# Turning attention weights on VectorE by 32x32 blocks instead of on TensorE, in a criss-cross attention kernel

## The chip, the cores and the metric

The kernel runs on one core of one Trainium2 chip. The metric is the device time of one execution in microseconds (us); a smaller one is better. "Profiled execution" means one execution that the hardware profiler recorded.

## The reference

For each of 8 images `x` (512 channels, 96 x 96) every pixel attends to its column and to its row. Cut to what matters:

```python
q = einsum('oc,bchw->bohw', Wq, x) + bq      # 64 channels
k = einsum('oc,bchw->bohw', Wk, x) + bk
v = einsum('oc,bchw->bohw', Wv, x) + bv      # 512 channels
energy_H = einsum('bchw,bcgw->bhwg', q, k) - 1e30 * eye      # along the column, itself masked
energy_W = einsum('bchw,bchv->bhwv', q, k)                   # along the row
att = softmax(concatenate([energy_H, energy_W], -1), -1)
out = gamma * (einsum(v, att_H) + einsum(v, att_W)) + x
```

All of it is float32.

## The kernel before

Each engine has its own program, written out by hand; semaphores order them, and every engine works strictly in the order of its own list. A batch is one image. Its columns and its rows are each cut into 24 chunks of `ROWS` = 4 (4 x 96 = 384 elements). The softmax is applied in two parts: exponentials of each chunk are stored to a scratch in HBM (`e_scratch`), with maxima `mx` and sums `zs` kept apart, and at the end of the energies `factors` works out one multiplier per pixel for columns and one for rows (`F`).

A batch then has two stages.

- **Column stage**, 24 chunks. SyncE loads a chunk of exponentials (`load_p`, 144 KB, into one of three buffers of `Pe`) and two pieces of 384 KB of the input with columns first (`load_xtc`, a ring of 6 pieces, `XT_r` and `XT_c`). GpSimd multiplies the chunk by its factors (`scale`, L390). TensorE turns each of the chunk's four 96 x 96 squares (`turn`, L867) into bank 7, ScalarE copies them to `Pt` (`copy_turned`, L499), and TensorE multiplies the input pieces by them (`attend_column`, L881: 16 products, 32 instructions in the trace). The four columns that come out go to `Y`, two by VectorE (L679), two by ScalarE (L505), each as four copies of 96 elements with a stride.
- **Row stage**. The same for the rows (`attend_row`, L900), whose results VectorE adds to `Y` (`add_row`, L687). Interleaved with it in iterations n = 0 to 23 runs the projection with Wv (`project`, L912, 48 products of 384 columns, the operand split in a high and a low part by `round_y` L516 and `low_y` L616), and VectorE's `finish` (L696) adds the bias and the input again.

Iterations 6 to 17 also carry the projection to q and k and the row energies of the next batch ("A chunks", two an iteration), iterations 18 to 22 its column energies ("B groups", five an iteration). At n = 23 `factors`, `factors_of_columns` and `factors_of_rows` make `F` for the next batch; the factors of rows are turned by TensorE (L861). For one chunk of energies VectorE does a maximum (L625), a subtraction into the ring `E` (L630) and a sum (L639), ScalarE the exponential (L486), GpSimd the mask (L381, columns only), SyncE the store (L217, L222).

A load waits until its buffer is free: `load_p(i)` waits for the turn of chunk i - 3 (semaphore `p_turned`), `load_xtc(i)` for the last product of piece i - 6. In SyncE's list of the column stage they stand as `load_p(g + 4)`, then the two pieces 2g + 6 and 2g + 7.

Of the kernel before, what the change touches and what calls it, by code (L numbers as in the profile page):

```python
# [7 lines left out]
AX_X = mybir.AxisListType.X  # L8
F32 = mybir.dt.float32
# [15 lines left out]
RBANKS = 3  # L25
# [24 lines left out]
def criss_cross_attention(nc, x, x_col, x_row, wqk_t, wv_t, bqk, bv, gamma, out):  # L50
# [8 lines left out]

    e_dram = nc.dram_tensor("e_scratch", (2, B, N, N, N), F32, kind="Internal").ap()  # L60

    ctx = ExitStack()
    with ctx:
# [10 lines left out]
        with ExitStack() as s1:  # L74
            XA = sb("XA", [P, 2, CT, CP], F32, s1)
            Sx = sb("Sx", [P, 2, CT, CP], F32R, s1)
            E = sb("E", [P, ERING, ROWS, N], F32, s1)
            KQ = sb("KQ", [P, POS], F32, s1)
            Kg = sb("Kg", [P, 2, CP], F32, s1)
            st = sb("st", [P, 4, N], F32, s1)  # L80
        with ExitStack() as s2:
# [17 lines left out]
        Pe = sb("Pe", [N, PRING, ROWS, N])  # L99
        Pt = sb("Pt", [P, 2, CP])  # L100
        Q = sb("Q", [P, 2, CP])
        mx = sb("mx", [N, 2, N])
        zs = sb("zs", [N, 2, N])
        F = sb("F", [N, 2, N])
# [6 lines left out]
        oc_ps, or_ps, proj_ps = (*bank[0:3], bank[5]), bank[0:RBANKS], bank[3:5]  # L111
        ec_ps, t_ps = bank[5:7], bank[7]
        st_ps, f_ps = bank[5], bank[6]
# [14 lines left out]
        def turns(a):  # L128
            return 2 if a == 0 else 1

# [18 lines left out]
        f_turned, f_made = sem("f_turned"), sem("f_made")  # L149
        p_in = [sem(f"p_in{j}") for j in range(PRING)]  # L150
        p_scaled, p_turned, pt_made = sem("p_scaled"), sem("p_turned"), sem("pt_made")
# [11 lines left out]
        by_pe = (x_half_used, qk_summed, e_summed, p_turned, o_summed, proj_summed)  # L163
        by_act = (x_hi_made, kq_evicted, q_gathered, e_exped, pt_made, c_moved_act, y_hi_made)
        by_dve = (x_lo_made, e_maxed, e_shifted, z_summed, c_moved_dve, r_added, y_lo_made, out_made, f_made)
# [3 lines left out]
        def past(s, n):  # L169
            return n + START[s]  # L170
# [28 lines left out]
        def _(sp):  # L199
# [15 lines left out]
            def store_row_energies(a, m):  # L215
                sp.wait_ge(e_exped, past(e_exped, e_no(a, m)))
                sp.dma_start(e_dram[1, a, :, m * ROWS:(m + 1) * ROWS, :], E[0:N, m % ERING, :, :])\  # L217
                    .then_inc(e_stored[m % ERING], 16)

            def store_column_energies(a, g):  # L220
                sp.wait_ge(c_masked, past(c_masked, a * CHUNKS + g + 1))
                sp.dma_start(e_dram[0, a, :, g * ROWS:(g + 1) * ROWS, :], E[0:N, g % ERING, :, :])\  # L222
                    .then_inc(e_stored[g % ERING], 16)

            def load_p(b, i):
# [3 lines left out]
                sp.dma_start(Pe[:, i % PRING, :, :], e_dram[along, b, :, n * ROWS:(n + 1) * ROWS, :])\  # L229
# [128 lines left out]
        def _(pool):  # L358
# [19 lines left out]
            def mask(a, g):  # L378
                pool.wait_ge(e_exped, past(e_exped, e_no(a, CHUNKS + g)))
                at = E[0:N, g % ERING, :, :]  # L380
                nc.gpsimd.affine_select(out=at, in_=at, compare_op=ALU.not_equal, fill=0.0, base=0,  # L381
                                        pattern=[[0, ROWS], [-1, N]], channel_multiplier=1).then_inc(c_masked, 1)

            def scale(b, i):
                along, n = i // CHUNKS, i % CHUNKS
                if n == 0:
                    pool.wait_ge(f_made, past(f_made, b * 2 + along + 1))
                pool.wait_ge(p_in[i % PRING], past(p_in[i % PRING], 16 * (b * (2 * CHUNKS // PRING) + i // PRING + 1)))
                f = F[:, along, n * ROWS:(n + 1) * ROWS].unsqueeze(2).to_broadcast((N, ROWS, N))
                nc.gpsimd.tensor_tensor(Pe[:, i % PRING, :, :], Pe[:, i % PRING, :, :], f, ALU.mult)\  # L390
                    .then_inc(p_scaled, 1)
# [62 lines left out]
        def _(act):  # L454
# [28 lines left out]
            def exponentials(a, i):  # L483
                act.wait_ge(e_shifted, past(e_shifted, e_no(a, i)))
                at = E[0:N, i % ERING, :, :]
# [10 lines left out]
            def copy_turned(b, i):  # L496
                act.wait_ge(p_turned, past(p_turned, p_no(b, i)))
                act.wait_ge(o_summed, past(o_summed, o_no(b, (i - 2) * ROWS + ROWS - 1)))
                nc.scalar.activation(Pt[0:N, i % 2, :], t_ps[0:N, 0:CP], ACT.Copy).then_inc(pt_made, 1)  # L499

            def move_column(b, i):
                act.wait_ge(o_summed, past(o_summed, o_no(b, i)))
                to = Y[:, 1:, :, :].rearrange("p n t (r w) -> p t n r w", w=N)[:, :, :, :, i]
                for t in range(CT):
                    last = nc.scalar.activation(  # L505
                        to[:, t, :, :], oc_ps[i % CBANKS][:, t * N:(t + 1) * N].rearrange("p (n r) -> p n r", r=ROWS),
                        ACT.Copy)
                last.then_inc(c_moved_act, 1)
# [8 lines left out]

            def factors(a):
                act.wait_ge(st_step, a * 8 + 3)
                nc.scalar.activation(st[0:N, 1:3, :], st[0:N, 1:3, :], ACT.Exp).then_inc(st_exped, 1)  # L520

            def column_stage(b):
                copy_turned(b, 0)
# [500 lines left out]
```

## Time and profile before

| | |
|---|---|
| median of 3 runs | 3886.9 us (3885.88 to 3889.6) |
| profiled execution | 3887.74 us, its span 3885.9 us |
| TensorE matmul busy | 3809.0 us, 98% of the span |
| VectorE busy | 2430.1 us, 63% |
| ScalarE busy | 1662.6 us, 43% |
| GpSimd busy | 625.9 us, 16% |
| DMA | 874.33 MB, mean 225 GB/s |

Busy is the time in which an engine has an instruction running; for TensorE the instructions overlap, so the time from the start of one group to the next says more than the sum of durations. The span is the time from the first to the last instruction of the profiled execution.

### The profile page before, as it was taken

The page shows a single profiled execution, that of the slowest core. Times are in us where ns is not written, and L with a number is a line of the kernel's source. Part 1 is how long each engine was busy: PE and PEld are TensorE (multiplying, and loading weights), DVE is VectorE, ACT ScalarE, POOL GpSimd, SP SyncE. Part 2 cuts the span into 40 slices and gives each one's busy share as a digit, 9 for nine tenths or more (in the row PEclk, how much of TensorE's full clock was granted, in tenths as well). Part 3 has the DMA queues.
Part 4 walks back from the last instruction along what each step waited for, and adds up shares of the span by engine and source line. Part 5 has one row for each costly group of instructions (what it writes and reads, how often), then busy time and mean ns, then how long its engine had stood idle before and what let it go on. Part 6 is the DMA issues. An engine that isn't in the chain of part 4 may idle for free.

```text
span 3885.9 us, 72644 instructions
## 1 busy us (share of the span) xinstructions
PE 3809.0 (98%) x28440; PEld 3780.9 (97%) x28440; DVE 2430.1 (63%) x5084; ACT 1662.6 (43%) x3658; POOL 625.9 (16%) x793
## 2 busy tenths in 40 slices
PE   7799999999999999999999999999999999999999
PEld 7799999999999999999999999999999999999999
DVE  8646675466754677546684567845767456674554
ACT  8533454244542445424454244542444424444111
POOL 0410023100221003210032100320004200042000
PEclk9899999999999999999999999999999999999999
DMA  7687768777687775977759677597775977668665
GB/s 257 168 220 248 245 209 221 220 248 248 198 232 223 247 238 195 240 225 239 249 184 246 223 247 241 194 240 226 240 243 183 240 234 248 224 197 239 208 205 167
DMA packets 256803, 874.33 MB, mean 225 GB/s; under 512 B 34256, under 2 KB 108496, under 8 KB 256464
## 3 DMA queue, kind: packets, MB, share of 16 engines
q1 hardware_dynamic: 256464, 869.67, 72.4%
q8 instruction: 230, 3.77, 0.4%
q14 instruction: 109, 0.89, 0.1%
HBM read 661.92 MB, written 207.62 MB: 224 GB/s over the span
## 4 chain that ended last, share of the span: by engine, by line
PE 94%; DVE 5%; issue 1%; ACT 1%; DMA 0%; POOL 0%; SPq 0%; DVEq 0%; ACTq 0%; POOLq 0%
PE bank L912 41%; PE bank L881 18%; PE bank L900 17%; PE bank L830 9%; PE bank L867 3%; PE bank L849 3%; PE bank L840 3%; DVE Sx L611 1%; DVE E L630 1%; DVE mx L625 1%; DVE zs L639 1%; DVE Sx_first L611 0%; DVE Sy L616 0%; DVE Y L696 0%; DMA XT_c<-in_x_col 0%
## 5 line engine op out<-in xcount | busy, mean ns | idle before, releaser
L912 PE MATMUL bank<-Sy,Wv_hi 128*128 128x384 f32 x6144 | 1596.3, 340 | 11.9 <-DVE Sy L616 11.9
L912 PEld LDWEIGHTS bank<-Sy,Wv_hi 128*128 128x128 f32 x6144 | 1088.7, 189 | 13.1 <-issue 13.1
L912 PE MATMUL bank<-Sy,Wv_lo 128*128 128x384 f32 x3072 | 1029.7, 335 | 0.0
L696 DVE SCALAR_TENSOR_TENSOR Y<-bank,bv_sb,Y 128x384 f32<-128x384 f32 x768 | 471.9, 614 | 872.2 <-PE bank L912 871.6
L390 POOL TENSOR_TENSOR Pe<-Pe,F 96x384 f32<-96x384 f32 x384 | 320.1, 835 | 2634.9 <-DMA Pe<-e_scratch 2601.2
L900 PE MATMUL bank<-Pt,XT_r 128*128 128x96 f32 x6144 | 725.0, 275 | 7.8 <-ACT Y L505 5.4
L900 PEld LDWEIGHTS bank<-Pt,XT_r 128*128 128x128 f32 x6144 | 705.0, 192 | 10.8 <-issue 6.6
L516 ACT ACTIVATE Sy<-Y 128x768 fp32r<-128x768 f32 x384 | 302.8, 835 | 897.2 <-PE bank L912 862.2
L679 DVE COPY Y<-bank 128x96 f32<-128x96 f32 x1536 | 317.9, 321 | 442.7 <-PE bank L881 442.7
L912 PEld LDWEIGHTS bank<-Sy,Wv_lo 128*128 128x128 f32 x3072 | 577.2, 188 | 0.0
L505 ACT ACTIVATE Y<-bank 128x96 f32<-128x96 f32 x1536 | 322.2, 360 | 373.4 <-PE bank L881 373.4
L687 DVE TENSOR_TENSOR Y<-bank,Y 128x384 f32<-128x384 f32 x768 | 393.7, 548 | 31.7 <-PE bank L900 31.7
L616 DVE TENSOR_TENSOR Sy<-Y,Sy 128x768 fp32r<-128x768 f32 x384 | 367.2, 958 | 33.8 <-ACT Sy L516 33.8
L830 PE MATMUL bank<-Sx,Wqk_hi 128*128 128x384 f32 x1440 | 375.7, 342 | 12.3 <-DVE Sx L611 12.3
L486 ACT ACTIVATE E<-E 96x384 f32<-96x384 f32 x384 | 200.2, 521 | 401.4 <-DVE E L630 401.2
L881 PE MATMUL bank<-Pt,XT_r 128*128 128x96 f32 x3072 | 366.6, 276 | 0.0
L881 PE MATMUL bank<-Pt,XT_c 128*128 128x96 f32 x3072 | 364.3, 275 | 1.5 <-issue 1.3
L881 PEld LDWEIGHTS bank<-Pt,XT_r 128*128 128x128 f32 x3072 | 355.8, 193 | 0.0
L881 PEld LDWEIGHTS bank<-Pt,XT_c 128*128 128x128 f32 x3072 | 353.2, 192 | 2.1 <-issue 1.8
L611 DVE TENSOR_TENSOR Sx<-XA,Sx 128x768 fp32r<-128x768 f32 x348 | 321.1, 964 | 1.5 <-ACT Sx L471 1.5
L471 ACT ACTIVATE Sx<-XA 128x768 fp32r<-128x768 f32 x348 | 274.8, 837 | 6.2 <-DMA XA<-in_x 2.0
L479 ACT ACTIVATE KQ<-bank,bqk_sb 128x384 f32<-128x384 f32 x192 | 111.6, 581 | 370.8 <-PE bank L830 369.2
(62 smaller groups left out, 3219.2 us busy)
## 6 DMA issues: line engine op xcount, KB each, us to landing
XT_r<-in_x_row SPq DMA_DIRECT2D x384, 384.0 KB, 5.5
Y<-in_x SPq DMA_DIRECT2D x192, 768.0 KB, 6.1
out<-Y SPq DMA_DIRECT2D x192, 768.0 KB, 3.6
XA<-in_x SPq DMA_DIRECT2D x180, 768.0 KB, 7.0
XT_r<-in_x_col SPq DMA_DIRECT2D x192, 384.0 KB, 6.7
XT_c<-in_x_col SPq DMA_DIRECT2D x192, 384.0 KB, 6.2
e_scratch<-E SPq DMA_DIRECT2D x384, 144.0 KB, 2.6
Pe<-e_scratch SPq DMA_DIRECT2D x384, 144.0 KB, 7.4
```

The costliest lines, as they stand in the source:

```text
L390: nc.gpsimd.tensor_tensor(Pe[:, i % PRING, :, :], Pe[:, i % PRING, :, :], f, ALU.mult)\
L505: last = nc.scalar.activation(to[:, t, :, :], oc_ps[i % CBANKS][:, t * N:(t + 1) * N].rearrange("p (n r) -> p n r", r=ROWS), ACT.Copy)
L516: nc.scalar.activation(Sy[:, 0, cts, :], Y[:, n + 1, cts, :], ACT.Copy).then_inc(y_hi_made, 1)
L611: nc.vector.tensor_tensor(sx(a, m)[:, 1, cts, :], xa(a, m)[:, cts, :], sx(a, m)[:, 0, cts, :].bitcast(F32), ALU.subtract).then_inc(x_lo_ma ...
L616: nc.vector.tensor_tensor(Sy[:, 1, halves[h], :], Y[:, n + 1, halves[h], :], Sy[:, 0, halves[h], :].bitcast(F32), ALU.subtract).then_inc(y ...
L679: last = nc.vector.tensor_copy(to[:, t, :, :], oc_ps[i % CBANKS][:, t * N:(t + 1) * N].rearrange("p (n r) -> p n r", r=ROWS))
L687: nc.vector.tensor_tensor(at, or_ps[i % RBANKS][:, 0:CT * N].rearrange("p (t n) -> p t n", t=CT), at, ALU.add).then_inc(r_added, 1)
L696: nc.vector.scalar_tensor_tensor(at, proj_ps[c % 2][:, 0:CP], bv_sb[:, c:c + 1], at, op0=ALU.add, op1=ALU.add).then_inc(out_made, 1)
L830: last = nc.tensor.matmul(ps[:, 0:CP], w[:, ct, :], sx(a, m)[:, lo, ct, :], start=(ct == 0 and n == 0), stop=(ct == CT - 1 and n == 2))
L881: last = nc.tensor.matmul(oc_ps[i % CBANKS][:, ct * N:(ct + 1) * N], column_piece(j)[:, u, ct * P:(ct + 1) * P], Pt[:, g % 2, r * N:(r + 1 ...
L900: last = nc.tensor.matmul(or_ps[i % RBANKS][:, ct * N:(ct + 1) * N], XT_r[:, j % RRING, u, ct * P:(ct + 1) * P], Pt[:, n % 2, r * N:(r + 1 ...
L912: last = nc.tensor.matmul(proj_ps[c % 2][:, 0:CP], w[:, ct, at], Sy[:, lo, ct, :], start=(ct == 0 and k == 0), stop=(ct == CT - 1 and k == 2))
```

## The change

- The scratch is laid out as `(2, B, CHUNKS, BLOCKS, N, ROWS * BLOCK)`, with `BLOCK` = 32 and `BLOCKS` = 3. `E` holds a chunk as three blocks of 4 x 32 elements. The store of a chunk writes each partition as three pieces of 512 bytes, where it was one of 1536 bytes. The load reads 1536 contiguous bytes for each partition, in an order that puts rows 3p to 3p + 2 of block b on partition 32b + p.
- In that order the turn of a whole chunk needs only 32x32 blocks to be transposed, each within its own 32 partitions. One VectorE instruction does it from `Pe` to `Pt`, and TensorE's four transposes and ScalarE's copy are gone. `load_p` now waits for VectorE's turn.
- Each column goes from its bank to `Y` by one copy of 384 elements, where it was four of 96.
- The factors get the same order of blocks: `F` holds three values for each, made by three products on TensorE for the columns and three for the rows (`turn_factors`, L907), with a chooser matrix that ScalarE writes (`choose_factors`).
- The row stage has 4 banks where it had 3. Its first bank is bank 7, free of turns now, and its first rows wait only for the copies out of their own bank.
- Near the end of a batch the last maximum and subtraction and the turn of the statistics stand elsewhere.

```diff
             def load_p(b, i):
                 along, n = i // CHUNKS, i % CHUNKS
                 sp.wait_ge(p_turned, past(p_turned, p_no(b, i - PRING)))
                 e_landed(sp, b, n if along else CHUNKS + n)
-                sp.dma_start(Pe[:, i % PRING, :, :], e_dram[along, b, :, n * ROWS:(n + 1) * ROWS, :])\
+                sp.dma_start(Pe[:, i % PRING, :],
+                             e_dram[along, b, n, :, :, :].rearrange("b (p q) x -> (b p) (q x)", q=BLOCKS))\
                     .then_inc(p_in[i % PRING], 16)
...
             def store_row_energies(a, m):
                 sp.wait_ge(e_exped, past(e_exped, e_no(a, m)))
-                sp.dma_start(e_dram[1, a, :, m * ROWS:(m + 1) * ROWS, :], E[0:N, m % ERING, :, :])\
+                sp.dma_start(e_dram[1, a, m, :, :, :].rearrange("b i x -> i b x"),
+                             E[0:N, m % ERING, :].rearrange("p (b x) -> p b x", b=BLOCKS))\
                     .then_inc(e_stored[m % ERING], 16)
...
-            def copy_turned(b, i):
-                act.wait_ge(p_turned, past(p_turned, p_no(b, i)))
-                act.wait_ge(o_summed, past(o_summed, o_no(b, (i - 2) * ROWS + ROWS - 1)))
-                nc.scalar.activation(Pt[0:N, i % 2, :], t_ps[0:N, 0:CP], ACT.Copy).then_inc(pt_made, 1)
...
+            def turn(b, i):
+                dve.wait_ge(p_scaled, past(p_scaled, p_no(b, i)))
+                dve.wait_ge(o_summed, past(o_summed, o_no(b, (i - 2) * ROWS + ROWS - 1)))
+                nc.vector.transpose(Pt[0:N, i % 2, :].rearrange("j (r p q) -> j q r p", r=ROWS, q=BLOCKS),
+                                    by_block(Pe[:, i % PRING, :])).then_inc(p_turned, 1)
 
             def move_column(b, i):
                 dve.wait_ge(o_summed, past(o_summed, o_no(b, i)))
                 to = Y[:, 1:, :, :].rearrange("p n t (r w) -> p t n r w", w=N)[:, :, :, :, i]
-                for t in range(CT):
-                    last = nc.vector.tensor_copy(
-                        to[:, t, :, :], oc_ps[i % CBANKS][:, t * N:(t + 1) * N].rearrange("p (n r) -> p n r", r=ROWS))
-                last.then_inc(c_moved_dve, 1)
+                nc.vector.tensor_copy(to, oc_ps[i % CBANKS][:, 0:CT * N].rearrange("p (t n r) -> p t n r", t=CT, r=ROWS))\
+                    .then_inc(c_moved_dve, 1)
...
             def column_stage(b):
+                turn(b, 0)
+                take_factors(b, 1)
...
                 for g in range(CHUNKS):
+                    turn(b, g + 1)
                     move_column(b, g * ROWS)
                     move_column(b, g * ROWS + 2)
...
-            def turn(b, i):
-                pe.wait_ge(p_scaled, past(p_scaled, p_no(b, i)))
-                pe.wait_ge(pt_made, past(pt_made, p_no(b, i - 1)))
-                for r in range(ROWS):
-                    last = nc.tensor.transpose(t_ps[0:N, r * N:(r + 1) * N], Pe[:, i % PRING, r, :], ident[:, :])
-                last.then_inc(p_turned, 1)
...
+            def turn_factors(a, along):
+                pe.wait_ge(f_ready, a * 2 + along + 1)
+                if not along:
+                    pe.wait_ge(f_chooser, a + 1)
+                for q in range(BLOCKS):
+                    last = nc.tensor.matmul(f_ps[along][:, q * N:(q + 1) * N], Kg[0:N, along, q * N:(q + 1) * N],
+                                            ident[:, :] if along else st[0:N, 1, :], start=True, stop=True)
+                last.then_inc(f_turned, 1)
...
             def attend_row(b, n, r):
...
-                if i < RBANKS:
-                    pe.wait_ge(c_moved_act, past(c_moved_act, (b + 1) * (N // 2)))
-                    pe.wait_ge(c_moved_dve, past(c_moved_dve, (b + 1) * (N // 2)))
+                if i == 0:
+                    pe.wait_ge(f_made, past(f_made, b * 2 + 2))
+                elif i < RBANKS:
+                    moved = c_moved_dve if i % 2 else c_moved_act
+                    pe.wait_ge(moved, past(moved, (b + 1) * (N // 2) - (RBANKS - 1 - i) // 2 - (1 - i % 2)))
```

In the lists of the engines the change stands as follows. First TensorE at the start of the first column stage, before (`ident,Pe` is a turn, `Pt,XT_r` and `Pt,XT_c` are `attend_column`):

```order
L861 MATMUL bank<-ident,st 96x96
L867 MATMUL bank<-ident,Pe 96x96 x8
L881 MATMUL bank<-Pt,XT_r 128x96 x16
L867 MATMUL bank<-ident,Pe 96x96 x4
L881 MATMUL bank<-Pt,XT_r 128x96 x8
L881 MATMUL bank<-Pt,XT_c 128x96 x8
L867 MATMUL bank<-ident,Pe 96x96 x4
```

and after:

```order
L900 MATMUL bank<-ident,zs_r 96x96
L907 MATMUL bank<-st,Kg 96x96 x3
L907 MATMUL bank<-ident,Kg 96x96 x3
L922 MATMUL bank<-Pt,XT_r 128x96 x24
L922 MATMUL bank<-Pt,XT_c 128x96 x24
```

Nothing stands between the chunks of the stage any more; six small products for the factors stand ahead of it.

Next VectorE at the end of batch 0's row stage and in the column stage that follows, before (L696 is `finish`, the rows with `st` are the factors):

```order
L665 RECIPROCAL st<-st 96x96
L668 TENSOR_TENSOR F<-st 96x96
L669 TENSOR_TENSOR st<-st 96x96
L696 SCALAR_TENSOR_TENSOR Y<-bank,bv_sb,Y 128x384
L673 COPY F<-bank 96x96
L696 SCALAR_TENSOR_TENSOR Y<-bank,bv_sb,Y 128x384
L679 COPY Y<-bank 128x24x4 x192
```

and after:

```order
L691 RECIPROCAL st<-st 96x96
L693 TENSOR_TENSOR st<-st 96x96
L694 TENSOR_TENSOR Kg<-st 96x288
L729 SCALAR_TENSOR_TENSOR Y<-bank,bv_sb,Y 128x384 x2
L701 COPY F<-bank 96x288
L729 SCALAR_TENSOR_TENSOR Y<-bank,bv_sb,Y 128x384
L707 STREAM_TRANSPOSE Pt<-Pe 96x3x128
L701 COPY F<-bank 96x288
L707 STREAM_TRANSPOSE Pt<-Pe 96x3x128
L713 COPY Y<-bank 128x4x24x4 x2
L707 STREAM_TRANSPOSE Pt<-Pe 96x3x128
```

Both factors now pass through TensorE before they reach `F`, and a turn stands ahead of each pair of column copies.

## Rows read from the trace of the kernel before

**Rows 1.** The page: busy time of the engines, and the last chain by line

```profile
PE 3809.0 (98%) x28440; PEld 3780.9 (97%) x28440; DVE 2430.1 (63%) x5084; ACT 1662.6 (43%) x3658; POOL 625.9 (16%) x793
...
PE bank L912 41%; PE bank L881 18%; PE bank L900 17%; PE bank L830 9%; PE bank L867 3%; PE bank L849 3%; PE bank L840 3%; DVE Sx L611 1%; DVE E L630 1%; DVE mx L625 1%; DVE zs L639 1%; DVE Sx_first L611 0%; DVE Sy L616 0%; DVE Y L696 0%; DM
```

**Rows 2.** Windows: column stage, A chunks, B groups; engines, PEclk, DMA share, GB/s

```profile
1100.00:1190.00 90.00, 90.00 (x832) 90.00 (x831) 38.08 (x184) 45.76 (x207) 20.07 (x24) 1.00 0.99 257
...
1280.00:1490.00 210.00, 209.70 (x1459) 208.53 (x1458) 146.24 (x234) 98.65 (x153) 12.30 (x14) 1.00 0.72 236
1490.00:1565.00 75.00, 74.85 (x581) 74.35 (x580) 63.60 (x117) 41.66 (x59) 33.76 (x47) 1.00 0.60 191
```

**Rows 3.** The chain that ended last, column stage: start, length, what

```profile
1115.56 3.59 PE bank L881 x32
1119.15 0.33 PE bank L867 x4
1119.48 3.57 PE bank L881 x32
```

**Rows 4.** Groups by form: busy us, mean ns, idle before and releaser

```profile
L390 POOL TENSOR_TENSOR Pe<-Pe,F 96x384 f32<-96x384 f32 x384 | 320.1, 835 | 2634.9 <-DMA Pe<-e_scratch 2601.2 <-DVE F L668 33.7
...
L679 DVE COPY Y<-bank 128x96 f32<-128x96 f32 x1536 | 317.9, 321 | 442.7 <-PE bank L881 442.7
...
L639 DVE TENSOR_REDUCE zs<-E 96x4 f32<-96x384 f32 x384 | 207.9, 541 | 12.4 <-POOL E L381 6.4
...
L499 ACT ACTIVATE Pt<-bank 96x384 f32<-96x384 f32 x384 | 191.4, 498 | 52.4 <-PE bank L867 50.3
L867 PE MATMUL bank<-ident,Pe 96*96 96x96 f32 x1536 | 190.8, 246 | 5.7 <-ACT Pt L499 4.7 <-POOL Pe L390 1.0
```

**Rows 5.** Timeline of the column stage of batch 2

```profile
1099.77 3.74 PE L881 MATMUL bank<-Pt,XT_r 128*128 128x96 f32 x32
...
1112.58 0.83 DVE L679 COPY Y<-bank 128x96 f32<-128x96 f32 x4 [1.29 <-PE bank L881]
...
1158.37 1.39 PE L881 MATMUL bank<-Pt,XT_r 128*128 128x96 f32 x11
```

**Rows 6.** Windows within the same column stage; the last two are DMA share, GB/s

```profile
1106.00:1124.00 18.00, 18.00 (x168) 18.00 (x168) 7.45 (x36) 9.39 (x45) 3.78 (x5) 1.00 1.04 273
1124.00:1148.00 24.00, 24.00 (x224) 24.00 (x223) 10.19 (x50) 12.25 (x55) 5.76 (x7) 1.00 1.04 257
1148.00:1190.00 42.00, 42.00 (x390) 42.00 (x389) 17.96 (x88) 21.32 (x98) 9.05 (x11) 1.00 0.94 246
```

**Rows 7.** Tile XT_r, the one load at 1148.6, and its landing

```profile
L239 SPq DMA_DIRECT2D XT_r<-in_x_col x1: 312/312/312, 1148.6 to 1148.6; - x1
...
DMA to landing us min/median/max: 7.2/7.2/7.2
```

**Rows 8.** Load of weights in the same stage: tile Pe, one load

```profile
L229 SPq DMA_DIRECT2D Pe<-e_scratch x1: 371/371/371, 1111.8 to 1111.8; - x1
...
DMA to landing us min/median/max: 9.0/9.0/9.0
```

**Rows 9.** Timeline at the start of batch 2's row stage

```profile
1194.47 3.78 PE L900 MATMUL bank<-Pt,XT_r 128*128 128x96 f32 x32 [0.79 <-ACT Y L505]
...
1196.50 0.31 SPq L247 DMA_DIRECT2D XT_r<-in_x_row  x1
```

**Rows 10.** Timeline of the handover from batch 2's rows to batch 3's columns

```profile
1573.65 0.29 PE L861 MATMUL bank<-ident,st 96*96 96x96 f32 x1 [0.71 <-DVE st L669]
...
1576.12 0.62 DVE L696 SCALAR_TENSOR_TENSOR Y<-bank,bv_sb,Y 128x384 f32<-128x384 f32 x1 [1.83 <-PE bank L912]
...
1577.42 3.74 PE L881 MATMUL bank<-Pt,XT_r 128*128 128x96 f32 x32
```

**Rows 11.** DMA queue, whole span, then 128 to 141 us (mostly stores): packets, MB, share

```profile
q1 hardware_dynamic: 256464, 869.67, 72.4%
...
q1 hardware_dynamic: 801, 1.29, 33.6%
```

More of the change, by code:

```diff
@@ L24 @@
 CBANKS = 4
-RBANKS = 3
+RBANKS = 4
+BLOCK = 32
+BLOCKS = N // BLOCK
 A_FIRST, A_LAST = 6, 17
@@ L129, in turns, with mx, zs, by_row @@
             return 2 if a == 0 else 1
+        def mx(along):
+            return mx_r[:, :] if along else mx_c[0:N, :]
+        def zs(along):
+            return zs_r[:, :] if along else zs_c[0:N, :]
+        def by_row(at):
+            return at.rearrange("p (b r f) -> p r b f", b=BLOCKS, r=ROWS)
+        def by_block(at):
+            return at.rearrange("p (b r f) -> p b r f", b=BLOCKS, r=ROWS)
+        def per_block(at):
+            return at.rearrange("k (p q) -> k q p", q=BLOCKS).unsqueeze(2).to_broadcast((N, BLOCKS, BLOCKS, BLOCK))
         def column_piece(i):
@@ L589, in prologue @@
                     exponentials(0, CHUNKS + g)
+                act.wait_ge(ident_made, 2)
+                choose_factors(0)
                 factors(0)
@@ L622, in shift @@
                 ps = src[0:N, 0:CP].rearrange("p (r n) -> p r n", r=ROWS)
-                m = mx[:, along, n * ROWS:(n + 1) * ROWS]
+                m = mx(along)[:, n * ROWS:(n + 1) * ROWS]
                 dve.wait_ge(e_summed, past(e_summed, e_no(a, i)))
+                if i == CHUNKS and before:
+                    out_landed(dve, a - 1, KG_SLOT)
                 nc.vector.tensor_reduce(m, ps, AX_X, ALU.max).then_inc(e_maxed, 1)
@@ L721, in row_stage @@
                     turn_now = more and n == CHUNKS - 1
+                    if turn_now:
+                        shift(b + 1, 2 * CHUNKS - 1)
+                        sum_z(b + 1, 2 * CHUNKS - 2)
+                        factors(b + 1)
                     finish(b, n, 0)
@@ L733, in row_stage @@
                         sum_z(b + 1, 2 * CHUNKS - 1)
-                        factors(b + 1)
+                        factors_ready(b + 1)
                     finish(b, n, 1)
@@ L761, in row_stage @@
                         add_row(b, n + 2, 1)
-                    if b_now:
+                    if b_now and CHUNKS - 1 not in b_now:
                         shift(b + 1, CHUNKS + b_now[3])
@@ L796, in prologue @@
                 for g in range(CHUNKS):
-                    shift(0, CHUNKS + g)
+                    shift(0, CHUNKS + g, before=False)
                     if g:
@@ L928, in row_stage @@
                 for n in range(2):
-                    turn(b, CHUNKS + n + 1)
                     for r in range(ROWS):
@@ L942, in row_stage @@
                         column_energies(b + 1, b_now[0])
-                    if turn_now:
+                    if more and n == CHUNKS - 2:
                         turn_stats(b + 1)
```

153 lines of the change are left out of this document (77 added, 76 removed).

## The prediction

> **What bounds the kernel now.** I read the page first. TensorE's matmuls are busy for 98% of the span and the last chain is almost only TensorE's lines [rows 1]: projections L912, L881 and L900, q and k L830, and 3% for L867, the turns. VectorE stands at 63%. But busy shares are averages, so next come the windows by stage [rows 2]. In all three TensorE has no idle time to speak of. In the column stage VectorE is busy 38 of 90 us, in the A chunks 146 of 210, in the B groups 64 of 75. So work taken off TensorE is worth its full time wherever nothing else stands close behind. The same rows say what does: in the column stage the DMA engines are busy 0.99 of the time.
>
> The chain within the column stage [rows 3] shows the period of one chunk: 3.57 us of attention and 0.33 us of turn, 3.90 together. Note that the groups [rows 4] give 246 ns for one transpose, four of them nearly 1 us: they overlap. The chain gives what they cost the path, 0.33 us for a chunk.
>
> **The turns.** There are 8 x 48 = 384 of them. Two in each batch lie in the handover between batches and are costed there. The other 46 are each 0.33 us of TensorE's own time, with no wait around them: 46 x 0.33 = 15.2 us a batch. This term holds where the other engines keep up, which the next paragraphs check.
>
> **VectorE's new load.** No row shows a VectorE transpose. The nearest is the sum L639, which reads the same 96x384 tile of `E` in SBUF at one element a step: 541 ns [rows 4]; I take 0.55 us. Below that I see no reason to go. Upwards, if each of its blocks started like an instruction of its own, four of L679's 321 ns would be 1.28 us. The column copy: four run in 0.83 us from first start to last end [rows 5], one instruction on the same elements and stride should not be longer; between 0.55 and 0.83 us. In the column stage VectorE then has 2 x 0.83 + 0.55 = 2.2 us of 3.57, and 2.9 with the worst turn. ScalarE loses its copy L499 of 498 ns and three starts in four. Neither binds. In the A chunks VectorE is busy 0.70 of the time; one turn in about 17.5 us adds 0.03. The tight place is the B groups: 63.6 of 75 us, 0.85. A turn falls in only three of their five iterations (n = 18 to 20) of some 16 us each, so 0.55 makes 0.88 and 1.28 makes 0.93. Over that window VectorE is idle for 11.4 us, and TensorE for 0.15. I cost it at nothing; if that cover were gone it would be 3 x 0.55 x 7 = 12 us over the kernel, and this is kept in the range.
>
> **The loads of the column stage.** Here I do not take the whole gain. A chunk needs two pieces of 384 KB and 144 KB of weights, 934 thousand bytes: in 3.90 us that is 239 GB/s, in 3.57 us 262 GB/s. The windows [rows 6] show 273 GB/s at a share of 1.04 (backlog from the start of the stage), then 257 at 1.04, then 246 at 0.94. So what the engines can deliver with this pattern is between about 255 and 275 GB/s, and the new demand lies inside. How late does that make TensorE? The piece issued at 1148.6 needs 7.2 us [rows 7] and lands at 1155.8. It belongs to chunk 15: the ring has six pieces, and TensorE begins it at 1158.37 now [rows 5]. Without turns chunk 15 would begin at 1099.77 + 15 x 3.57 = 1153.3. As the engines were saturated up to there, an earlier issue would not bring it sooner: TensorE comes 2.5 us late. After that the share is below 1 and the delivery about equals the demand, so I leave it at a loss of 2.5 us a batch. Its bounds: nothing, if a faster consumer gets faster delivery; and at most the whole gain of the stage, 23 turns x 0.33 = 7.6 us, if 239 GB/s is all there is.
>
> The Trainium skill, "DMA: Bandwidth & Descriptors", section "Where 436 GB/s comes from", puts the limit for one core's HBM traffic at about 358 GB/s. By it 262 GB/s would leave room and the term would be 0. The row with 273 GB/s at a full share speaks against that for this stage.
>
> **The start of the row stage.** TensorE idles 0.79 us for ScalarE's last column copy [rows 9]. With bank 7 for the first row that wait goes. The load of the fourth row piece is issued only 2 us after this start, so what follows can catch up with it; I take 0.6 of the 0.79.
>
> **The handover.** Now L861 waits 0.71 us for the factors [rows 10]. After, TensorE does three small products there (less than the 0.9 us that wait and transpose take) and three more before the columns. The first `attend_column` must wait for VectorE: `finish` L696 ends at 1576.74, and the new turn behind it, 0.55 and a signal, would end where the stage starts now, 1577.42. The projection ahead of it ends perhaps 0.3 us sooner: 0.3 us gained. The three products for the row factors lie under that wait. The bound is 1 us either way. At the end of batch 0's energies, where no projection covers it, the same chain occurs once: nothing, within 2 us.
>
> **The sum.** 15.2 - 2.5 + 0.6 + 0.3 = 13.6 us a batch, 108.8 us in eight. From the profiled execution, 3887.7 - 108.8 = 3778.9. The median of the runs is 0.8 lower: **3778 us**.
>
> **Smaller packets.** Stores now go out as 288 packets of 512 bytes instead of 96 of 1536. In the stretch with nearly only stores, 801 packets of that mix took 33.6% of 16 engines' 13 us [rows 11]: 87 ns each. If a 512-byte packet cost as much, a store would take 192 x 87 / 16 = 1.04 us more of the engines. Two stores in an A iteration bring the share of 0.72 to 0.84, five in a B iteration the 0.60 to 0.92. Under 1, so nothing for the sum. The column stage has no stores.
>
> **The rivals.**
> - *Delivery follows.* The 2.5 us go to zero: 3778 - 20 = 3758. For it: packets in the row stage move as fast at a share of 0.72. Against: the 1.04 shares. Chance 0.17.
> - *The column stage is the DMA's.* It keeps its present length and only the row stage gains: 3778 + 8 x (7.6 - 2.5) = 3819. For it: a share of 0.99 over 90 us with 257 GB/s. Against: the share fell to 0.94 as the backlog was worked off. Chance 0.22.
> - *Slower: the weights' loop.* `load_p(i + 3)` waits for VectorE's turn of chunk i. The loop of three buffers is turn, load 9.0 [rows 8], scale 0.83 [rows 4], and some 0.5 us of issue and signals: (0.55 + 9.0 + 0.83 + 0.5) / 3 = 3.63 us a chunk, hardly above 3.57. Behind a waiting turn in VectorE's list stand the column copies, and behind those TensorE's banks; in SyncE's list the pieces stand behind `load_p`. So it can feed itself: later turns, later loads. The row stage and the two small terms gain 8.5 us a batch; the column period must rise from 3.90 to 4.25 us to eat it, which takes a turn of 2.4 us, or loads of 10.9. Should both go to 1.3 and 12, the period is 4.87 and the time 3887 + 8 x (24 x 0.97 - 8.5) = 4005. Against: in the saturated stretch the loads are at 9.0 and decline. Chance 0.06.
> - *The stores choke the B groups.* The ring `E` has four buffers; a late store holds VectorE's subtraction and then TensorE. It bites when five stores' extra time exceeds the free 6.4 us of a 16 us iteration. Seven batches have about five such iterations, 34 in all, so to eat 108.8 us each must lose 3.2: (6.4 + 3.2) / 5 = 1.9 us a store, 160 ns for each of its 192 added packets. The kernel's mean packet of 3.4 KB takes 175 ns (72.4% of 16 x 3886 us over 256464 packets [rows 11]); at that price an iteration has 9.6 + 10.5 = 20.1 us of DMA, and the time is 3887 - 109 + 34 x 4 = 3914. Against: 87 ns for the smaller ones. Chance 0.05.
>
> The Trainium skill, "Perfetto Trace Analysis", section "DMA Optimizations", says that DMAs under 2 KB have significant overhead for each transfer and asks for batching into larger ones; that is this last rival's rule. By the 87 ns it has no room to decide.
>
> **How the numbers follow.** The forecast has a chance of 0.50. The range of 80% reaches from the second case with some gain at the edges, 3748, to the third with the 12 us of the B groups not quite on top, 3828. Its own range is 3765 to 3795. What a measurement of this kernel can tell from no change is about 0.2%, 8 us. The first three cases and part of the last are faster: 0.91; same 0.02; slower 0.07.
>
> **What would show it.** After the change: no L867 in the chain, and chunks of attention that follow at 3.57 us in the second half of the column stage; in its first half TensorE waits on DMA for XT_c or XT_r, 2 to 3 us a batch; the transpose near 0.55 us; the wait of 0.79 at the row stage gone; a plain iteration of the row stage 0.33 us shorter. Wrong would be: TensorE waiting for the turn's semaphore within the stage, with loads of weights above 10 us, or for VectorE's subtraction in the B groups.

## The result and the profile after

| | before | after |
|---|---|---|
| median | 3886.8 us | 3755.4 us (3753.5 to 3758.3, 4 runs) |
| profiled execution | 3887.74 us | 3755.24 us, its span 3753.5 us |
| VectorE busy | 63% | 72% |
| DMA share of the queue | 72.4% | 75.8% |

The ratio is 0.9661, 95% interval 0.9645 to 0.9678: 131 us less, where 109 were forecast. Four more runs of the same kernel on another chip gave 3757.2 us, ratio 0.9666 [0.9653, 0.9680].

The page of the changed kernel, the lines that answer to [rows 1, 4, 11]: busy times, the queue's packets, the last chain by line, and three groups.

```profile
PE 3680.6 (98%) x26992; PEld 3663.1 (98%) x26992; DVE 2686.3 (72%) x4324; ACT 1526.3 (41%) x2130; POOL 644.8 (17%) x793
...
q1 hardware_dynamic: 330192, 869.67, 75.8%
...
PE bank L955 42%; PE bank L922 18%; PE bank L943 17%; PE bank L873 10%; PE bank L883 3%; PE bank L892 3%; DMA XT_r<-in_x_row 1%; DVE E L657 1%; DVE Sx L636 1%; DVE Sx_first L636 0%; DVE zs_c L667 0%; DVE Sy L641 0%; DVE mx_c L652 0%; DVE mx_r L652 0%; DVE zs_r L667 0%
...
L530 ACT ACTIVATE Y<-bank 128x384 f32<-128x384 f32 x384 | 325.4, 847 | 436.7 <-PE bank L922 436.7
L713 DVE COPY Y<-bank 128x384 f32<-128x384 f32 x384 | 318.0, 828 | 217.0 <-PE bank L922 198.4
...
L707 DVE STREAM_TRANSPOSE Pt<-Pe 96x384 f32<-96x384 f32 x384 | 267.3, 696 | 29.2 <-POOL Pe L422 2.7
```

The turns have left TensorE's chain (L922 is now `attend_column`, L943 `attend_row`, L955 `project`), and nothing else of size has come into it. VectorE's turn takes 696 ns. The column copy as one instruction takes 828 ns, the same as four pieces did [rows 5].

Windows of the changed kernel, columns as in [rows 2]: three in batch 2's column stage, then the A chunks and the B groups.

```profile
1070.00:1090.00 20.00, 19.30 (x172) 19.04 (x171) 12.40 (x16) 8.90 (x11) 4.14 (x5) 1.00 1.03 274
1090.00:1110.00 20.00, 20.00 (x182) 20.00 (x181) 13.55 (x18) 9.40 (x12) 4.74 (x6) 1.00 1.04 267
1110.00:1150.00 40.00, 40.00 (x358) 39.92 (x358) 26.01 (x33) 19.10 (x23) 8.97 (x12) 1.00 1.04 261
...
1250.00:1450.00 200.00, 200.00 (x1378) 199.70 (x1377) 147.35 (x240) 90.33 (x135) 13.06 (x16) 1.00 0.75 247
1450.00:1515.00 65.00, 65.00 (x507) 64.84 (x506) 59.52 (x109) 35.48 (x51) 31.36 (x44) 1.00 0.59 181
```

The share of 1.04 that stood only in the first half of the stage before [rows 6] now lasts to its end, at 261 to 274 GB/s. VectorE is busy 0.74 and 0.92 in the two stretches of the row stage, the DMA 0.75 and 0.59. The chain through the same column stage shows what that costs:

```profile
1066.64 0.84 issue
1067.48 18.27 PE bank L922 x160
1085.74 0.70 issue
1086.45 68.43 PE bank L922 x608
1154.88 0.71 PE bank L943 x6
```

768 instructions (384 products) in 87.4 us, and one hole of 0.70 us after the first 160, that is, ahead of the eleventh piece and the sixth chunk. That piece's load was issued at 1076.8 and took 9.5 us. The other stages look alike: from one chunk's first product to the next it is 3.57 us nearly everywhere. Of the holes, one of 3.1 us stands between the first and the second chunk of batch 0 (2.6 before), and those of the other batches stand between the starts of the second and the sixth chunk, but for a few tenths near the end of batches 2 and 5.

Cut into stretches by the first instruction of each line (means over the eight batches, us; the forecast's terms put in the same stretches; 24 of the 46 turns fall in the first one):

| stretch | before | after | gained | forecast |
|---|---|---|---|---|
| first column product to first row product | 95.34 | 87.28 | 8.06 | 24 x 0.33 + 0.6 - 2.5 = 6.0 |
| from there to the first projection | 7.51 | 7.68 | -0.17 | 0.33 |
| from there to the next batch | 375.07 (7 batches) | 366.51 | 8.57 | 21 x 0.33 + 0.3 = 7.2 |
| last batch, from there to the end of the last product | 290.23 | 280.86 | 9.37 | 6.9 |

Eight batches give 132.4 us, the difference of the two profiled executions (132.5).

### The profile page after: what moved, and what is told of

Read it like the earlier page. It is cut to its first block, busy times and chain, and to the rows that moved or that the text cites. A ratio compares the mean times of both kernels' runs of the same rounds, so it can differ in the third digit from the quotient of the medians.

```text
span 3753.5 us, 67076 instructions
## 1 busy us (share of the span) xinstructions
PE 3680.6 (98%) x26992; PEld 3663.1 (98%) x26992; DVE 2686.3 (72%) x4324; ACT 1526.3 (41%) x2130; POOL 644.8 (17%) x793
## 3 DMA queue, kind: packets, MB, share of 16 engines
q1 hardware_dynamic: 330192, 869.67, 75.8%
## 4 chain that ended last, share of the span: by engine, by line
PE 93%; DVE 4%; DMA 1%; issue 1%; ACT 0%; POOL 0%; DVEq 0%; SPq 0%; ACTq 0%; POOLq 0%
PE bank L955 42%; PE bank L922 18%; PE bank L943 17%; PE bank L873 10%; PE bank L883 3%; PE bank L892 3%; DMA XT_r<-in_x_row 1%; DVE E L657 1%; DVE Sx L636 1%; DVE Sx_first L636 0%; DVE zs_c L667 0%; DVE Sy L641 0%; DVE mx_c L652 0%; DVE mx_r L652 0%; DVE zs_r L667 0%
## 5 line engine op out<-in xcount | busy, mean ns | idle before, releaser
L955 PE MATMUL bank<-Sy,Wv_hi 128*128 128x384 f32 x6144 | 1593.6, 340 | 12.9 <-DVE Sy L641 11.9
L955 PEld LDWEIGHTS bank<-Sy,Wv_hi 128*128 128x128 f32 x6144 | 1087.2, 188 | 15.2 <-issue 13.1
L955 PE MATMUL bank<-Sy,Wv_lo 128*128 128x384 f32 x3072 | 1027.6, 335 | 0.0
L943 PE MATMUL bank<-Pt,XT_r 128*128 128x96 f32 x6144 | 717.4, 274 | 2.7 <-DMA XT_r<-in_x_row 2.4
L943 PEld LDWEIGHTS bank<-Pt,XT_r 128*128 128x128 f32 x6144 | 713.7, 192 | 4.1 <-DMA XT_r<-in_x_row 4.0
L955 PEld LDWEIGHTS bank<-Sy,Wv_lo 128*128 128x128 f32 x3072 | 576.6, 188 | 0.0
L530 ACT ACTIVATE Y<-bank 128x384 f32<-128x384 f32 x384 | 325.4, 847 | 436.7 <-PE bank L922 436.7
L713 DVE COPY Y<-bank 128x384 f32<-128x384 f32 x384 | 318.0, 828 | 217.0 <-PE bank L922 198.4
L720 DVE TENSOR_TENSOR Y<-bank,Y 128x384 f32<-128x384 f32 x768 | 393.3, 547 | 9.5 <-PE bank L943 9.0
L922 PE MATMUL bank<-Pt,XT_r 128*128 128x96 f32 x3072 | 358.1, 277 | 8.1 <-issue 7.8
L922 PEld LDWEIGHTS bank<-Pt,XT_r 128*128 128x128 f32 x3072 | 351.6, 193 | 9.9 <-issue 9.2
L922 PE MATMUL bank<-Pt,XT_c 128*128 128x96 f32 x3072 | 355.5, 275 | 4.1 <-issue 4.1
L922 PEld LDWEIGHTS bank<-Pt,XT_c 128*128 128x128 f32 x3072 | 349.0, 192 | 5.4 <-issue 4.8
L707 DVE STREAM_TRANSPOSE Pt<-Pe 96x384 f32<-96x384 f32 x384 | 267.3, 696 | 29.2 <-POOL Pe L422 2.7
```

What stands on the lines that cost most here:

```text
L530: nc.scalar.activation(to, oc_ps[i % CBANKS][:, 0:CT * N].rearrange("p (t n r) -> p t n r", t=CT, r=ROWS), ACT.Copy).then_inc(c_moved_act, 1)
L713: nc.vector.tensor_copy(to, oc_ps[i % CBANKS][:, 0:CT * N].rearrange("p (t n r) -> p t n r", t=CT, r=ROWS))\
L720: nc.vector.tensor_tensor(at, or_ps[i % RBANKS][:, 0:CT * N].rearrange("p (t n) -> p t n", t=CT), at, ALU.add).then_inc(r_added, 1)
L922: last = nc.tensor.matmul(oc_ps[i % CBANKS][:, ct * N:(ct + 1) * N], column_piece(j)[:, u, ct * P:(ct + 1) * P], Pt[:, g % 2, r * N:(r + 1 ...
L943: last = nc.tensor.matmul(or_ps[i % RBANKS][:, ct * N:(ct + 1) * N], XT_r[:, j % RRING, u, ct * P:(ct + 1) * P], Pt[:, n % 2, r * N:(r + 1 ...
L955: last = nc.tensor.matmul(proj_ps[c % 2][:, 0:CP], w[:, ct, at], Sy[:, lo, ct, :], start=(ct == 0 and k == 0), stop=(ct == CT - 1 and k == 2))
```

## The experiments

Kernels are edits of the changed one unless said otherwise.

**The same kernel again**, for its spread.

> The changed kernel once more, as the mark for the others on the same chip: 3755 us, within 3 us.

3757.2 us (3753.4 to 3761.4), as told above.

**Three banks in the row stage.**

```diff
-RBANKS = 4
+RBANKS = 3
-        ... or_ps ... = ... (bank[7], *bank[0:3]), ...
+        ... or_ps ... = ... (bank[7], *bank[0:2]), ...
...
```

> The changed kernel with three banks for the rows instead of four (the first still bank 7, the same early start). Theory: the fourth bank took away stray waits of TensorE for VectorE's additions, which in the kernel before made single iterations of the row stage 0.1 to 0.5 us longer, about 1 us a batch; so 5 to 10 us above the changed kernel, 3760 to 3765. Rival: those waits came from turns that stood in TensorE's list and are gone with them; then no difference, 3755.

Measured 3785.6 us (3784.1 to 3788.4), ratio 0.9740 [0.9727, 0.9753]: 30 us slower than the changed kernel, three times the most that either theory had. The chain through one A iteration shows where. First the changed kernel: row products and what follows them.

```profile
1282.69 3.54 PE bank L943 x32
...
1300.17 3.54 PE bank L943 x32
```

The same place with three banks, the chain, and then the timeline of both engines (L720 is `add_row`).

```profile
1287.87 3.77 PE bank L943 x32
...
1305.58 3.77 PE bank L943 x32
```

```profile
1287.71 3.93 PE L943 MATMUL bank<-Pt,XT_r 128*128 128x96 f32 x32
...
1288.51 0.60 DVE L729 SCALAR_TENSOR_TENSOR Y<-bank,bv_sb,Y 128x384 f32<-128x384 f32 x1
1289.04 0.94 DVE L641 TENSOR_TENSOR Sy<-Y,Sy 128x768 fp32r<-128x768 f32 x1
1289.90 0.55 DVE L720 TENSOR_TENSOR Y<-bank,Y 128x384 f32<-128x384 f32 x1
```

And the kernel before, the chain at that place:

```profile
1289.93 0.33 PE bank L867 x4
1290.26 3.57 PE bank L900 x32
...
1307.78 0.33 PE bank L867 x4
1308.11 3.57 PE bank L900 x32
```

with its timeline (L687 is `add_row` there):

```profile
1289.77 0.49 PE L867 MATMUL bank<-ident,Pe 96*96 96x96 f32 x4
...
1290.10 2.51 PE L900 MATMUL bank<-Pt,XT_r 128*128 128x96 f32 x21
...
1291.96 0.55 DVE L687 TENSOR_TENSOR Y<-bank,Y 128x384 f32<-128x384 f32 x1
```

With three banks the fourth row of a chunk needs the bank of its first, and that comes free when `add_row` ends. On VectorE this stands behind `finish` and half a `low_y`, which follow the last projection. So the release has a fixed distance from the projection: 1289.90 + 0.55 = 1290.45. TensorE would need it 24 instructions after 1287.71, at 3.54 / 32 = 0.11 us each at 1290.37, and the weight load ahead of that still 0.2 us sooner. The block takes 3.77 us in place of 3.54, and the iteration 17.71 in place of 17.48 (1305.58 - 1287.87, 1300.17 - 1282.69). Before, the release came at 1291.96 + 0.55 = 1292.51, and by the same count TensorE needed it at 1290.10 + 2.66 = 1292.76, less 0.2 for the weight load: it was there by 0.05 us. The turn between projection and rows was the 0.33 us in which VectorE got ahead, so three banks were enough, and taking it away uncovered the wait. The added time is 0.05 us in a plain iteration and 0.24 in eleven of a batch's twelve A iterations, with strays in some batches; summed from the first projection to the next batch (the last one to its end), 2.9 to 5.2 us a batch, 31 us in all. The view of waits names only 9.4 us of them.

**The turn alone**: three banks, the old wait for all column copies, and four copies for each column.

```diff
-RBANKS = 4
+RBANKS = 3
-                nc.vector.tensor_copy(to, oc_ps[i % CBANKS][:, 0:CT * N]...)
+                for t in range(CT):
+                    last = nc.vector.tensor_copy(to[:, t, :, :], oc_ps[i % CBANKS][:, t * N:(t + 1) * N]...)
-                elif i < RBANKS:
-                    ... the bank's own copy
+                if i < RBANKS:
+                    ... all column copies
```

ScalarE's column copies are undone in the same way, and the row banks are banks 0 to 2 again. What stays of the change is the turn on VectorE with the layout and the factors that it needs, and the new places of a few instructions at a batch's end.

> The changed kernel with three things undone: three banks of the rows, the old wait for all column copies at the start of the row stage, and four copies for each column. Theory: what is left, the turn on VectorE, gives nearly all: the start of the row stage costs 0.8 us a batch again, 6 us, the banks 5 to 10, the copies nothing, so 3766 to 3771. Rival: four copies and a turn together make VectorE late in the column stage (2 x 0.83 us of copies and 0.7 of turn in 3.57 leaves 1.2), and the stage gets longer by more than 0.1 us a chunk, 20 us and more, 3790.

Measured 3802.0 us (3799.3 to 3803.0), ratio 0.9780 [0.9767, 0.9794], above both expectations. So of the 131 us the turn and what it needs bring 85, the fourth bank 30, and the two other edits together 16, taken off in this order. With three banks here too, the stretch from projection to next batch is 370.39 us, as in the run before (370.53): the loss is the number of banks, whichever they are. The 16 us lie in the column stretch, mean 89.27 us against 86.97. Here is its end in batch 2:

```profile
1164.66 0.83 ACT L531 ACTIVATE Y<-bank 128x96 f32<-128x96 f32 x4 [0.94 <-PE bank L927]
1164.74 0.69 DVE L710 STREAM_TRANSPOSE Pt<-Pe 96x384 f32<-96x384 f32 x1
...
1165.75 1.44 PE L948 MATMUL bank<-Pt,XT_r 128*128 128x96 f32 x11 [1.12 <-ACT Y L531]
```

The waits of weight loads, whole span (us in total, times, longest), give the sum of that one wait:

```profile
PEld bank L948 <- DVE Pt L710: 10.2, 8, 1.4
```

The view puts it down to a turn, but the turn at 1164.74 is that of the second row chunk, for which the first row product does not wait; its own turn ran from 1161.15 to 1161.86. What TensorE waits for is ScalarE's last column copy, which ended at 1165.49. This is the old wait for all column copies, put back by this run: 1.3 us in each batch, 10.2 of the 16. Before, the same wait was 0.79 us [rows 9], with a turn of 0.33 ahead of it. The rest of the 16, longer column stages, has no cause shown, and no run takes the copies and the wait apart.

**A longer turn**: 0.54 us more of VectorE for each.

```diff
+                nc.vector.tensor_reduce(spare[:, i % 2, :], Pe[:, i % PRING, :]..., AX_X, ALU.max)
                 nc.vector.transpose(Pt[0:N, i % 2, :]..., by_block(Pe[:, i % PRING, :]))
```

> The changed kernel with one more VectorE instruction of 384 elements (a maximum that nobody reads, 0.54 us) ahead of each turn. Theory: VectorE has the room in the column stage and in the A chunks, and just so in the B groups: 3755 to 3760. Rival, the loop of the weights' three buffers: the 0.54 us come into turn, load, scale and turn again, 0.18 us a chunk of the column stage, 24 x 8 chunks, 35 us: 3790.

3760.7 us (3759.2 to 3767.9), ratio 0.9678 [0.9665, 0.9691]. The column stage keeps its length (mean 87.36 against 87.28). What is lost is 0.9 us a batch (once 1.3) between projection and next batch. Part of it is the handover: in batch 2 the columns wait 1.29 us for VectorE, where it was 0.84, since one more 0.54 us instruction stands ahead of the first turn. The rest was not traced. VectorE's load and the loop of the weights do not bind, or the loss would be the 35 us of the rival.

**How fast the column stage could be**: in the changed kernel and in that of before, each column's 4 products of 96 columns (16 in a chunk) became one of 384 columns, which leaves out most of the attention over columns and keeps every transfer, copy and turn.

```diff
-                for ct in range(CT):
-                    last = nc.tensor.matmul(oc_ps[i % CBANKS][:, ct * N:(ct + 1) * N],
-                                            column_piece(j)[:, u, ct * P:(ct + 1) * P], Pt[:, g % 2, r * N:(r + 1) * N], ...)
+                nc.tensor.matmul(oc_ps[i % CBANKS][:, 0:CP], column_piece(j)[:, u, 0:P], Pt[:, g % 2, :], ...)
```

> The changed kernel, but each column's 16 products in the column stage are one product of 384 columns with the first 128 channels (the rest of that part of the computation is left out), so that TensorE needs some 1.3 us a chunk instead of 3.57 and the stage goes as fast as its loads or VectorE let it. Theory A, the prediction's: the DMA engines deliver 255 to 275 GB/s and no more in this stage, so a chunk takes 3.4 to 3.7 us. Theory B: the share of 1.04 was a queue that the ring of six pieces keeps full and not a ceiling, and they can go clearly faster, over 300 GB/s: a chunk under 3.1 us (VectorE alone would allow about 2.4).

> The same cut in the kernel before. If the ceiling is a matter of the input pieces, a chunk takes as long as in the changed kernel. If the contiguous scratch of the changed kernel is what lets its loads go faster than I had read off the kernel before, this one takes longer, 3.7 us a chunk or more, at the 239 to 255 GB/s that I took as the floor.

3736.6 us and 3813.9 us, one run each. Windows within batch 2's column stage, first of the one made from the changed kernel:

```profile
1066.00:1140.00 74.00, 61.44 (x166) 27.77 (x164) 45.90 (x63) 34.48 (x42) 17.36 (x21) 1.00 1.04 267
```

and of the one made from that of before:

```profile
1085.00:1160.00 75.00, 72.04 (x254) 35.81 (x252) 34.77 (x170) 41.61 (x189) 17.27 (x21) 1.00 1.04 271
```

TensorE's weight loads fill only 28 of 74 us, and the stage still takes 84.7 us (86.5 in the other; means of eight, single stages 82.4 to 87.5 and 85.2 to 89.1). This is the DMA's own pace: 22.4 MB in 84.7 us, 265 GB/s, 3.53 us a chunk, where the products need 3.57. That is theory A; nothing under 3.1 us a chunk came. The changed kernel's 87.3 stands 2.6 above this stage and 1.5 above the 85.8 us of its products. The 3.57 us of TensorE and the 3.53 of the DMA lie so near that whichever is late first sets the stage, and with TensorE nearly out of the way there are only those 2.6 us a batch to gain. The 1.8 us between the two cut kernels lie within the spread of single stages, so they say nothing sure of the layout.

**The layout alone**: before, with a scratch contiguous by chunks.

```diff
-    e_dram = nc.dram_tensor("e_scratch", (2, B, N, N, N), ...)
+    e_dram = nc.dram_tensor("e_scratch", (2, B, CHUNKS, N, ROWS, N), ...)
```

> The kernel before with only the scratch laid out by chunks, so that a chunk's 144 KB are contiguous in HBM (stores and loads still 1536 bytes for each partition). If the layout speeds up the loads, the few waits for them at the start of the column stage go, some 1 us a batch: 3879 to 3885. If not, no difference: 3887.

3887.4 us, ratio 1.0001 [0.9993, 1.0010]: nothing.

**Stores in whole partitions**, of rows as shown and of columns likewise.

```diff
-                sp.dma_start(e_dram[1, a, m, :, :, :].rearrange("b i x -> i b x"),
-                             E[0:N, m % ERING, :].rearrange("p (b x) -> p b x", b=BLOCKS))\
+                sp.dma_start(e_dram[1, a, m, :, :, :].rearrange("b (p q) x -> (b p) (q x)", q=BLOCKS), E[0:N, m % ERING, :])\
```

> The changed kernel with stores of the energies that write each partition's 1536 bytes in one piece, 96 packets in place of 288; the weights then stand in the wrong order in the scratch, so the values of the output are others, while all instructions and all other transfers stay. It prices the 512-byte packets of the stores. Theory (they cost nothing where they stand, since the DMA share is 0.59 to 0.75 in the row stage): 3755 us, within 0.2%. Rival (TensorE is held by stores through the ring E now and then): 3745 us or less.

3756.4 us, ratio 0.9662 [0.9649, 0.9676]: the 512-byte packets cost nothing here, in stretches with a DMA share of 0.59 to 0.75.

**The first turn earlier**: ahead of the last `finish` of the batch before, since the columns wait 0.84 us for it (chain above).

```diff
             def column_stage(b):
-                turn(b, 0)
+                if b == 0:
+                    turn(b, 0)
...
                     if turn_now:
                         take_factors(b + 1, 0)
+                        turn(b + 1, 0)
                     finish(b, n, 3)
```

> The changed kernel with the first turn of a batch ahead of the last finish of the batch before in VectorE's list. The first column product now waits 0.84 us for finish (0.6 us) and turn (0.67 us); the weights are scaled 1.2 us earlier than the turn starts. Theory: TensorE starts 0.6 to 0.8 us sooner in seven batches, 4 to 6 us less: 3750. Rival: the sooner start only meets the loads of the stage's first pieces, which are late already, and nothing is gained.

3757.7 us (3754.1 to 3767.6), ratio 0.9674 [0.9661, 0.9687]: nothing. The stretch from projection to next batch falls by 0.99 us, somewhat more than the wait promised (366.51 to 365.52), and the column stage grows by 0.76 (mean 88.04). Its chain at the start of batch 2's stage:

```profile
1067.22 5.36 PE bank L924 x48
1072.58 0.84 issue
1073.42 2.00 PE bank L924 x16
```

48 instructions are the first three pieces, and the hole is ahead of the fourth, the first in `XT_c`. `XT_c` shares its memory with `Sy`, so it can be loaded only when the last projection is done; and in SyncE's list the store of the last output chunk stands ahead of it, as the timeline of the changed kernel shows:

```profile
1065.97 0.67 PE L907 MATMUL bank<-ident,Kg 96*96 96x96 f32 x6
1066.17 0.62 DVE L729 SCALAR_TENSOR_TENSOR Y<-bank,bv_sb,Y 128x384 f32<-128x384 f32 x1 [1.58 <-PE bank L955]
1066.70 0.67 DVE L707 STREAM_TRANSPOSE Pt<-Pe 96x384 f32<-96x384 f32 x1
1066.82 0.36 SPq L291 DMA_DIRECT2D out<-Y  x1
...
1067.22 0.43 SPq L269 DMA_DIRECT2D XT_c<-in_x_col  x1
...
1067.48 1.77 PE L922 MATMUL bank<-Pt,XT_r 128*128 128x96 f32 x14 [0.84 <-issue]
```

The load takes 5.5 us to land (1072.7) and is due at 1067.48 + 5.36 = 1072.84: just in time. With an earlier start it is late by what was won.

**That store later**, alone and with the earlier turn.

```diff
+LATE = 23
...
                 for g in range(CHUNKS):
                     load_p(b, g + PRING + 1)
+                    if b and g == LATE:
+                        store_out(b - 1, CHUNKS - 1)
...
-                    store_out(b, n)
+                    if n < CHUNKS - 1 or not more:
+                        store_out(b, n)
```

> The changed kernel, with the store of each batch's last output chunk (768 KB, slot 0 of Y) moved in SyncE's list from the end of the row stage to iteration 23 of the next column stage. In the changed kernel it is issued 0.4 us ahead of the first XT_c load, at the moment when three pieces have to be fetched that could not be fetched earlier because they share memory with Sy; at some 270 GB/s it holds the DMA engines for 2.9 us. Theory A (what keeps the column stage 1 to 1.5 us above its 85.75 us of products is the backlog at its start): the pieces land up to 2.9 us sooner, the stage falls to about 86.0 us, seven times 1.2 us are gained, 3747 us; up to 0.5 us a batch can be given back at the start of the row stage, where the store now runs beside the first row pieces. Rival B (the stage is as long as its bytes take, wherever they stand): the store is still in the stage, no change, 3755 us.

> Both edits: the store of the last output chunk late, as in the run before, and the first turn of a batch ahead of the last finish on VectorE, which started the column stage 0.98 us sooner and gave it all back inside the stage. Theory A (the backlog at the stage's start took it back): with the store out of the way most of that 1.0 us stays, 7 x (1.2 + 0.8) = 14 us, 3741 to 3745 us. Rival B (the stage's bytes set its end): 3755 us. In between (the three XT_c loads can't be issued before the projection's last product, so the earlier start is lost again, but the store's 1.2 us are kept): 3747 us.

Alone 3756.9 us (3753.7 to 3770.0), ratio 0.9672 [0.9657, 0.9687]: theory A had 3747. In its profiled execution four stages are free of holes, at 85.81 us; three others take 87.98, 88.22 and 90.79, the last with chunks of 3.6 to 4.8 us from its sixth on. So with this edit alone a stage may run without a hole or fall behind, and what decides it was not found. With both edits 3746.3 us (3743.0 to 3749.1), ratio 0.9637 [0.9624, 0.9651]. Batch 2's stage in the chain:

```profile
1064.54 0.26 PE bank L913 x3
1064.79 85.76 PE bank L928 x768
1150.55 1.00 PE bank L949 x9
```

Not one hole: 85.76 us for 768 instructions, and so (within 0.22 us) in all batches but the first. Its first `XT_c` load:

```profile
L270 SPq DMA_DIRECT2D XT_c<-in_x_col x1: 328/328/328, 1064.3 to 1064.3; - x1
...
DMA to landing us min/median/max: 3.7/3.7/3.7
```

> The same kernel as late_early once more, on another chip run, since its 3746.3 us stand only 9 us under the changed kernel and the late store alone gave nothing. If both edits together are really faster (column stages of 85.76 us in most batches and a start 0.98 us sooner), 3743 to 3749 us again; if it was chance in how the loads fall, 3753 to 3758 us, with column stages of 87 us.

3743.1 us (3740.2 to 3750.7), ratio 0.9633 [0.9620, 0.9646]. The mean of the two medians is 11.6 us under that of the changed kernel's two: each edit alone gives nothing, and together they make the version that beats both kernels. The first `XT_c` piece now lands in 3.7 us where it took 5.5, and the holes at the start of the stage are gone.

## Why the prediction came out as it did

- **The bound.** TensorE's own time, as said: the chain is still TensorE's almost throughout, and time taken off it shows in every stretch of the table but the second.
- **The turns, 0.33 us each.** Right in the column stage. In the row stage an iteration became 0.37 us shorter: 17.85 to 17.48 and 12.26 to 11.89. The row products themselves take 3.54 in place of 3.57 us (chains above). 21 turns make 0.8 us a batch.
- **"No wait around them."** This was true of the trace and stood in the prediction without its condition. In the row stage the turn was the slack that let three banks do. Had the change not brought a fourth, 30 of the 131 us would be missing. The prediction gave the fourth bank only the 0.79 us at the start of the row stage; the working never asked whether three would still do, so that the row stage came out near its forecast is, in this point, luck.
- **The DMA's lateness, 2.5 us a batch.** This is the step that missed most, in its size and in its place. The share did stay at 1.04 and TensorE did come to a piece late, but at the start of the stage, between the second and the sixth chunk, and not at chunk 15, where the working put it; there the chunks follow at 3.57 us. And the changed stage stands 87.28 - 85.76 = 1.5 us above its products. Before, 95.34 less 85.76 of products, 7.9 of turns and 0.7 of the wait at its end (5.4 us in seven batches) leaves 1.0 us that was lost already. The net term is 0.5, not 2.5. I took the landing of chunk 15's first piece as fixed, 56.0 us after the stage's start (1155.8 - 1099.77), "as the engines were saturated up to there". The same piece after the change:

```profile
L269 SPq DMA_DIRECT2D XT_r<-in_x_col x1: 312/312/312, 1113.5 to 1113.5; - x1
...
DMA to landing us min/median/max: 8.4/8.4/8.4
```

  It lands at 1121.9, that is 54.4 us after the start, 1.6 us sooner than in the stage of before. So the loads of before were held by their consumer, at a share of 1.04 too: asked sooner, the engines moved more (261 to 274 GB/s over the whole stage, where the second window of before had 257). What is left of the lateness is the backlog at the stage's start, as the two edits together show: with them it is gone. The term is 2.0 us a batch too large, 16 us of the 23 by which the forecast fell short. "Delivery follows" (3758) was the better case, and its 0.17 too little.
- **The start of the row stage**: the wait is gone (0.7), but the opening then waits for row pieces (4.0 us in eight batches), -0.17 where 0.33 stood. Together about 0.4 a batch less than the 0.6 and 0.33 that I took.
- **The handover, 0.3.** Batch 2's, from the last row block to the first column, became 0.15 us shorter. L861's wait of 0.71 [rows 10] is gone, and a wait of 0.84 for VectorE's `finish` and turn is in its place, as described.
- **The rest of the 8.57**: strays. Before, A iterations of 17.95, 18.33 and 18.17 us stood among those of 17.85, 0.9 us in batch 2; after, all twelve are 17.48. I had not priced them.
- **VectorE's load at nothing.** Holds with 0.70 us for 0.55; with 0.54 more (the longer turn) it costs 5 us, and still no wait for the turn within the stage. The rival of the weights' loop falls by the same run; in batch 2's column stage the loads of weights of the changed kernel took 8.0 us (median; 7.0 before), far from the 10.9 that it needed. The rival of the packets falls by the stores in whole partitions.

The Trainium skill, "DMA: Bandwidth & Descriptors", section "Where 436 GB/s comes from", has about 358 GB/s as the limit for one core. Here, with TensorE nearly out of the way and the engines' share at 1.04 or 1.05, 265 to 277 GB/s moved in the windows of the cut kernels. For these loads the measurement decides: a TensorE-bound stage at 262 GB/s of demand was already at its second bound.

## What to carry to other kernels

Work taken off the bounding engine may have been the slack of a neighbour: before counting it in full, look how far ahead of need each buffer comes free at that place, and by which engine's list. When one stage stands on two bounds at once, time it with the first bound cut away; and look for transfers that could stand elsewhere at the moment when its ring is empty, since an earlier start alone is given back there.

## What the runs showed of the hardware

- A VectorE transpose of 96x384 float32 by 32x32 blocks takes 696 ns where it reads in blocks and writes with a stride of three elements; a sum over the same elements 541.
- The last 48 products of the kernel took 10.14 us before and 8.58 after, in a stretch that the change does not touch. The chain of before, and windows (the granted clock is the third column from the end):

```profile
3860.93 8.39 PE bank L912 x48
...
3871.39 10.14 PE bank L912 x48
```

```profile
3869.30:3871.40 2.10, 0.02 (x2) 0.04 (x1) 1.74 (x3) 1.58 (x2) 0.00 (x0) 1.00 0.31 129
3871.40:3873.40 2.00, 2.00 (x9) 2.00 (x10) 0.71 (x1) 0.00 (x0) 0.00 (x0) 0.76 0.64 258
3873.40:3875.40 2.00, 2.00 (x7) 2.00 (x7) 0.62 (x1) 0.00 (x0) 0.00 (x0) 0.50 0.00 0
```

TensorE waited 2.1 us and came back, and the clock then fell to 0.50 of full speed, the lower level of 1.2 GHz, for about 3 us. After the change the same wait of 2.1 us stands there and the clock stays at 1.00. Over the profiled executions it came in both kinds (10.14 to 10.18 us in eight kernels, 8.58 in six), so 1.6 of the 132.5 us that the two profiled executions differ by need not be the change's. The three kernels without the change all showed 10.14 us or more, in one profiled execution each, so whether they ever escape it is not shown.
